# Attention of a two-layer kernel: heads placed in two halves of the rows, one DMA for the parts of a head, two groups projected at once, and all values at the beginning

## The reference

```
scores = q @ k.T * 16**-0.5          # (batch 2, head 16, 1024, 1024), causal
attn   = softmax(scores)
out    = (attn @ v) @ Wo (+ bo)
```

## Time and profile before

| | us |
|---|---|
| median of three runs | 2348.93 |
| profiled execution | 2359.97 |
| its span, first to last instruction | 2358.1 |
| granted TensorE clock, mean | 0.901 |

### The profile page before, as it was taken

One profiled execution on the slowest core, in us unless ns is written; L12 is line 12 of the kernel. 1 busy time (PEld: TensorE's weight loads), 2 busy tenths in 40 slices (PEclk: granted clock), 3 DMA queues, 4 the chain that ended last, 5 costly groups with the idle time before them and its releaser, 6 DMA issues. The chain is left out here.

```text
span 2358.1 us, 28715 instructions
## 1 busy us (share of the span) xinstructions
PE 1968.2 (83%) x9912; PEld 1308.5 (55%) x9912; DVE 1624.1 (69%) x3486; ACT 857.2 (36%) x1599; POOL 455.3 (19%) x324
## 2 busy tenths in 40 slices
PE   6899998699999988856867385646789999999998
PEld 4455554488888856433433242323345555469998
DVE  3788881444444354789999989996477888156775
ACT  2265563222222222430122111110325556336775
POOL 0011110623033030001101100110001111015775
PEclk9699998899999999978988697777869999989999
DMA  4122220311010010100000000000112222028885
GB/s 159 35 58 58 58 57 11 125 36 56 34 53 18 0 54 30 59 1 9 10 10 0 18 9 9 0 0 3 48 41 49 57 59 57 11 66 252 231 235 123
DMA packets 62849, 129.63 MB, mean 55 GB/s; under 512 B 22792, under 2 KB 33800, under 8 KB 59904
## 3 DMA queue, kind: packets, MB, share of 16 engines
q1 hardware_dynamic: 53120, 115.04, 16.3%
q0 software_dynamic: 8832, 12.16, 3.0%
q10 hardware_dynamic: 768, 0.79, 0.1%
HBM read 91.27 MB, written 10.98 MB: 43 GB/s over the span
## 5 line engine op out<-in xcount | busy, mean ns | idle before, releaser
L713 DVE CUSTOM_DVE_ANT_0 pair<-pair,a_mask 128x512 f32<-128x512 f32 (+3 forms) x768 | 409.6, 581 | 113.3 <-PE pair L561 110.1
L677 ACT ACTIVATE a_prob<-pair 128x512 f32<-128x512 f32 (+3 forms) x768 | 329.7, 496 | 248.6 <-PE pair L585 244.4
L561 PE MATMUL pair<-a_kx,a_qx 96*128 96x512 f32 (+3 forms) x768 | 255.2, 400 | 33.3 <-DMA a_qx<-a_comp 19.8
L585 PE MATMUL pair<-a_qx,a_kx 98*128 98x512 f32 (+3 forms) x768 | 267.3, 395 | 6.6 <-ACT a_prob L677 5.7
L956 DVE TENSOR_TENSOR m_h<-pair,m_g 128x512 f32<-128x512 f32 x96 | 66.4, 691 | 215.3 <-PE pair L779 214.6
L585 PEld LDWEIGHTS pair<-a_qx,a_kx 98*128 98x128 f32 x768 | 143.9, 194 | 118.6 <-ACT a_prob L677 81.2
L516 POOL TENSOR_SCALAR_AFFINE_SELECT a_prob<-a_prob 128x512 f32<-128x512 f32 x128 | 82.3, 643 | 644.8 <-ACT a_prob L677 644.8
L1338 PE MATMUL pair<-h_stream,r_w_kz 128*128 128x512 f32 x192 | 106.9, 712 | 116.6 <-DVE r_region L1744 113.3
L561 PEld LDWEIGHTS pair<-a_kx,a_qx 96*128 96x128 f32 x768 | 152.5, 205 | 91.6 <-DVE a_mx_raw L713 47.8
L777 PE MATMUL pair<-m_x_hi,m_w_lo 128*128 128x512 f32 x448 | 177.5, 396 | 26.4 <-POOL m_w_lo L841 24.2
L779 PE MATMUL pair<-m_x_lo,m_w_hi 128*128 128x512 f32 x448 | 176.3, 393 | 0.0
(11 more groups left out here) (307 smaller groups left out, 4126.9 us busy)
## 6 DMA issues: line engine op xcount, KB each, us to landing
mx_raw<-in_L_ffn_experts SPq DMA_DIRECT2D x69, 512.0 KB
m_raw<-in_L_cond_experts SPq DMA_DIRECT2D x18, 1024.0 KB, 4.8
a_kx<-a_comp SPq DMA_DIRECT2D x96, 128.0 KB, 2.4
a_qx<-a_comp SPq DMA_DIRECT2D x360, 32.0 KB, 2.0
a_factor<-a_inverses SPq DMA_DIRECT2D x56, 128.0 KB, 2.7
r_w_ring<-in_r_q_w SPq DMA_DIRECT2D x8, 512.0 KB, 4.0
m_raw<-in_L_cond_experts SPq DMA_DIRECT2D x6, 512.0 KB, 3.7
token_rows<-mx_h_rows SPq DMA_DIRECT2D x2, 1040.0 KB, 8.6
```

The source lines that it names most:

```text
L561: nc.tensor.matmul(first_bank[t % FR][:, 0:c1 - c0], qx[0:PRODUCT, m % 2, a, i * P:(i + 1) * P], kx[0:PRODUCT, m % 3, a // 2, c0:c1], star ...
L585: nc.tensor.matmul(score_bank[t % SR][:, q0:TT], kx[0:ROWS, n % 3, a // 2, j * P:(j + 1) * P], qx[0:ROWS, n % 2, a, h * TT + q0:(h + 1) * ...
L677: nc.scalar.activation(prob[:, i % RING, a, q0:TT], score_bank[t % SR][:, q0:TT], ACT.Exp, scale=SCALE).then_inc(s["b_exp"], 1)
L713: nc.vector.tensor_tensor_reduce(out=first_bank[t % FR][:, 0:cols], in0=first_bank[t % FR][:, 0:cols], in1=mask[:, m0:m0 + cols], scale=1. ...
```

## The change

Heads 0 and 2 of a group now lie in rows 0 to 63 of `qx` and `kx`, heads 1 and 3 in rows 64 to 127. Each has its three parts in 48 rows (50 with the maxima), with no zeros, and one DMA places the three parts of a head. For this `comp` holds four parts (upper, lower, upper, upper), of which ScalarE writes three, in two instructions. In the head, groups 0 and 1 are projected one after the other in banks of their own, the second through space of `prob`; group 0's keys are placed by half. All eight `v` blocks stand among group 0's 48 `first`, one behind every fifth, in four banks that are free there, and none is in a turn. ScalarE in place of VectorE copies values and maxima. The weight of the value matmul has 17 columns in place of 32. The ones of `kx` are set by GpSimd, before the keys come.

```diff
--- before.py
+++ after.py
-PRODUCT = 3 * 2 * HD
+VW = HD + 1
+PRODUCT = 3 * HD
 ROWS = PRODUCT + 2
...
-SMALL = (("max", 0, 1), None, None, ("qk", 2, 0), ("qk", 2, 1), ("max", 1, 0), ("v", 0, 0), None, None, None, None, None)
+SMALL = (("max", 0, 1), None, None, ("qk", 2, 0), ("qk", 2, 1), ("max", 1, 0), None, None, None, None, None, None)
...
 def before_turns():
 
     order = []
...
+        order += [("qk", 0, h), ("qk_use", 0, h), ("k_slots", 0, h), ("q_slots", 0, h)]
     for h in range(HALF):
-        order.append(("qk", 1, h))
-        firsts(MAX0 + 9 + 4 * h, MAX0 + 13 + 4 * h)
-        order.extend(finished("qk", 1, h))
-    firsts(MAX0 + 17, NF)
+        order += [("qk", 1, h), *finished("qk", 1, h)]
+    order.append(("q_slots", 1, 1))
+    values = [(pair, v) for pair in range(NG // 2) for v in range(2)]
+    for f in range(NF):
+        order.append(("first", 0, f))
...
+        if f % 5 == 2 and values:
+            order += [("v", *values[0]), ("v_use", *values[0])]
+            values = values[1:]
     order.append(("split", 0, 1))
     return order
...
+    early = {("qk", 0, 1): 0, ("qk", 1, 0): 1, ("qk", 1, 1): 2}
+    v_banks = [value_bank, *score_bank]
...
-        comp = c.sb(f"{tag}_comp", [P, 2, T], F32R, ctx=ctx)
+        comp = c.sb(f"{tag}_comp", [P, 4, T], F32R, ctx=ctx)
         kx = c.sb(f"{tag}_kx", [P, 3, PAIRS, T], F32R, ctx=ctx)
-        qx = c.sb(f"{tag}_qx", [P, 2, GH, T], F32R, ctx=ctx)
-        v_sb = c.sb(f"{tag}_v", [P, 4, QT, P], ctx=ctx)
+        qx = c.sb(f"{tag}_qx", [P, 2, PAIRS, T], F32R, ctx=ctx)
+        v_sb = c.sb(f"{tag}_v", [P, NG, QT, GH * VW], ctx=ctx)
...
+        second = prob[:, 0:2, :, :].rearrange("p x a t -> p (x a t)").rearrange("p (x t) -> p x t", x=4).bitcast(F32R)
+
+        def parts(m):
+            return second if m == 1 else comp[:, :, :]
+
+        def rows_of(a, n):
+            return slice(a % 2 * 64, a % 2 * 64 + n)
...
-                    for p in range(PAIRS):
-                        rows = slice(64 + p * 32, 96 + p * 32)
-                        for part, low in enumerate((0, 1, 0)):
-                            sp.dma_start(kx[part * 32:part * 32 + 32, m % 3, p, :].bitcast(F32), comp[rows, low, :].bitcast(F32))\
-                                .then_inc(s["k_in"], 16)
+                    t = slice(0, T) if h is None else half(h)
+                    for a in range(GH):
+                        rows = slice(64 + a * HD, 64 + a * HD + HD)
+                        sp.dma_start(kx[rows_of(a, PRODUCT), m % 3, a // 2, t].bitcast(F32), parts(m)[rows, 0:3, t].bitcast(F32))\
+                            .then_inc(s["k_in" if m else f"k_first{h}"], 16)
...
-                        for part, low in enumerate((0, 0, 1)):
-                            r0 = part * 32 + a % 2 * HD
-                            sp.dma_start(qx[r0:r0 + HD, m % 2, a, half(h)].bitcast(F32), comp[rows, low, half(h)].bitcast(F32))\
-                                .then_inc(s[f"q_in{h}"], 16)
+                        sp.dma_start(qx[rows_of(a, PRODUCT), m % 2, a // 2, half(h)].bitcast(F32),
+                                     parts(m)[rows, 1:4, half(h)].bitcast(F32))\
+                            .then_inc(s[f"q_in{h}" if m else f"q_first{h}"], 16)
...
-                    for a in range(GH):
-                        sp.dma_start(qx[PRODUCT:ROWS, m % 2, a, half(h)].bitcast(F32), stage[2 * a:2 * a + 2, :].bitcast(F32))\
+                    for x in range(2):
+                        sp.dma_start(qx[x * 64 + PRODUCT:x * 64 + ROWS, m % 2, :, half(h)].bitcast(F32),
+                                     stage[2 * PAIRS * x:2 * PAIRS * x + 2 * PAIRS, :].bitcast(F32))\
                             .then_inc(s[f"m_in{h}"], 16)
...
-                for a in range(GH):
-                    nc.gpsimd.memset(qx[:, 1, a, :].bitcast(F32), 0.0).then_inc(s["zero1"], 1)
...
+                for x in range(3):
+                    nc.gpsimd.memset(kx[:, x, :, :].bitcast(F32), 1.0).then_inc(s["ones"], 1)
...
-                    nc.tensor.matmul(first_bank[t % FR][:, 0:c1 - c0], qx[0:PRODUCT, m % 2, a, i * P:(i + 1) * P],
-                                     kx[0:PRODUCT, m % 3, a // 2, c0:c1], start=True, stop=True).then_inc(s["a_mm"], 1)
+                    r = rows_of(a, PRODUCT)
+                    nc.tensor.matmul(first_bank[t % FR][:, 0:c1 - c0], qx[r, m % 2, a // 2, i * P:(i + 1) * P],
+                                     kx[r, m % 3, a // 2, c0:c1], start=True, stop=True).then_inc(s["a_mm"], 1)
...
-                    nc.tensor.matmul(score_bank[t % SR][:, q0:TT], kx[0:ROWS, n % 3, a // 2, j * P:(j + 1) * P],
-                                     qx[0:ROWS, n % 2, a, h * TT + q0:(h + 1) * TT], start=True, stop=True)\
+                    r = rows_of(a, ROWS)
+                    nc.tensor.matmul(score_bank[t % SR][:, q0:TT], kx[r, n % 3, a // 2, j * P:(j + 1) * P],
+                                     qx[r, n % 2, a // 2, h * TT + q0:(h + 1) * TT], start=True, stop=True)\
                         .then_inc(s["b_mm"], 1)
...
-                        r = quadrant(a)
-                        last = nc.tensor.matmul(value_bank[r, q0:TT], v_sb[:, n % 4, j, r], prob[:, i % RING, a, q0:TT],
+                        r = slice(a * SLOT, a * SLOT + VW)
+                        last = nc.tensor.matmul(value_bank[r, q0:TT], v_sb[:, n, j, a * VW:(a + 1) * VW], prob[:, i % RING, a, q0:TT],
                                                 start=j == 0, stop=j == 4 * h + 3)
...
-                    nc.scalar.activation(comp[:, 0, half(h)], bank_of("qk", m, h), ACT.Copy).then_inc(s["hi"], 1)
...
+                    nc.scalar.activation(to[:, 2:4, :], bank_of("qk", m, h).unsqueeze(1).broadcast_to([P, 2, TT]), ACT.Copy)\
+                        .then_inc(s["hi"], 1)
+                    act.wait_ge(s["hi"], m * HALF + h + 1)
+                    nc.scalar.activation(to[:, 0, :], to[:, 2, :].bitcast(F32), ACT.Copy).then_inc(s["twin"], 1)
...
-                for a in range(GH):
-                    nc.vector.memset(qx[:, 0, a, :].bitcast(F32), 0.0).then_inc(s["zero0"], 1)
                 dve.wait_ge(s["mask"], 16)
```

More of the change, by code:

```diff
@@ L299, in turn @@
     closing = m == NG
-    order, found, uses = ([] if closing else [("q_slots", m, 1)]), 0, []
+    order, found, uses = ([("q_slots", m, 1)] if 1 < m < NG else []), 0, []
     for i in range(NS):
@@ L523, in take @@
                 def take(*entry):
-                    if used(*entry) > SB:
+                    if entry not in early and used(*entry) > SB:
                         pe.wait_ge(s["used"], used(*entry) - SB)
@@ L541, in v_projection @@
                     m = 2 * pair
-                    bank = take("v", pair, v)
+                    task = 2 * pair + v
+                    pe.wait_ge(s["used"], used("qk", 1, 1))
+                    if task >= len(v_banks):
+                        pe.wait_ge(s["v_used"], task - len(v_banks) + 1)
+                    bank = v_bank(pair, v)
                     for t in range(4):
@@ L648, in upper, with copy_values, copy_maxima @@
                     act.wait_ge(s["proj"], m * HALF + h + 1)
-                    if m and h == 0:
-                        act.wait_ge(s["k_in"], m * PAIRS * 3 * 16)
-                        act.wait_ge(s["q_in0"], m * GH * 3 * 16)
-                        act.wait_ge(s["q_in1"], m * GH * 3 * 16)
-                    nc.scalar.activation(comp[:, 0, half(h)], bank_of("qk", m, h), ACT.Copy).then_inc(s["hi"], 1)
+                    if m == 2 and h == 0:
+                        for x in range(HALF):
+                            act.wait_ge(s[f"k_first{x}"], GH * 16)
+                            act.wait_ge(s[f"q_first{x}"], GH * 16)
+                    if m > 2 and h == 0:
+                        for name in ("k_in", "q_in0", "q_in1"):
+                            act.wait_ge(s[name], (m - 1) * GH * 16)
+                    to = parts(m)[:, :, half(h)]
+                    nc.scalar.activation(to[:, 2:4, :], bank_of("qk", m, h).unsqueeze(1).broadcast_to([P, 2, TT]), ACT.Copy)\
+                        .then_inc(s["hi"], 1)
+                    act.wait_ge(s["hi"], m * HALF + h + 1)
+                    nc.scalar.activation(to[:, 0, :], to[:, 2, :].bitcast(F32), ACT.Copy).then_inc(s["twin"], 1)
+                def copy_values(pair, v):
+                    act.wait_ge(s["vp"], pair * 2 + v + 1)
+                    for x in range(2):
+                        last = nc.scalar.activation(
+                            v_sb[:, 2 * pair + x, 4 * v:4 * v + 4, :].rearrange("p t (a s) -> p t a s", s=VW)[:, :, :, 0:HD],
+                            v_bank(pair, v).rearrange("p (t x a s) -> p t x a s", t=4, x=2, s=HD)[:, :, x, :, :], ACT.Copy)
+                    last.then_inc(s["v_used"], 1)
+                def copy_maxima(m, h):
+                    act.wait_ge(s["t_mm"], m * HALF + h + 1)
+                    if h:
+                        act.wait_ge(s["m_in0"], (m + 1) * 2 * 16)
```

(11 more changed lines are left out.)

108 lines of the change are left out of this document (41 added, 67 removed).

## The result

The changed kernel takes 2405.51 us, the median of four runs, against 2352.66 before, the median of four. One of the four was disturbed (4644.01 us) and enters no ratio; the other three have 2390.92 to 2407.54, median 2403.47. The ratio is **1.022**, 95% interval 1.018 to 1.026: slower, where I had forecast 2258. The profiled execution took 2407.54, with a span of 2405.8 and a mean granted clock of 0.864, where it was 0.901.

A forecast was written before the change was run, and what follows sets the result against it. TensorE was taken to lead the turns, VectorE close behind at 31.3 of 37.2 us. Savings of 43.7 us in stage one and 47.7 in stage two, together 91.4, from the median 2348.93 gave 2258; range 2223 to 2300.

The forecast's parts named there:

- the likeness: Turns 1 to 5: would take 32.5 us, like the old turn 6 with TensorE 27.5 and VectorE 29.5 busy.
- TensorE then needs 32.9 - 1.8 - 4.6 = 26.5: Turns 1 to 5: TensorE's 32.9 us less 1.8 for the v projection and 4.6 for overlap, below VectorE's 29.2.
- First maximum: Head: VectorE's first maximum begins at 50.8 us, 6.1 us earlier.
- Rest of the head: Head after 50.8 us: 25.2 us of maxima, 0.9 of splits, 3.6 of waits; ends at 80.5 against 91.4.
- The rival with `v` blocks at half clock: Head: a v block takes 3.9 us, the sum loses 2 x 11 us, whole kernel 2280; chance 0.09.
- Turn 0: First turn of each stage: the 5.2 us wait for queries goes; about 33.5 us, 11 us less.
- VectorE's floor: Turns 1 to 5: VectorE busy 31.3 - 0.75 - 1.35 = 29.2 us a turn.
- Overlap of the halves: Turns: matmuls in opposite row halves run at once, 17.6 us become 13.0, 4.6 less, of which little is seen.
- The no-overlap rival: Turns: halves do not overlap, TensorE 31.1 us, turns 35.4, 54 us saved, whole kernel 2295; chance 0.17.
- Slower by bare weight loads: Turns: 44 same-half neighbours each pay a 0.19 us load, 8.4 a turn, turns about 43.8, whole kernel 2411; chance 0.05.
- Mode changes: Turns: TensorE switching between whole array and halves costs 0.085 us each, 0.34 a turn, within its slack.
- Closing turn: Last turn of each stage: no first there, each projection adds a change of tiling mode; +0.5 us.

The follow-up runs named there:

- e2: Kernel before the change, with first and scores stating 62 and 64 rows instead of 96 and 98, all in the lower half, no overlap; one execution, 2421.94 us.
- e5: Changed kernel, halves kept, with 62 and 64 rows stated instead of 48 and 50; 2330.23 us in one execution, 2333.43 as median of five, ratio 0.991.
- e12: e1 with first stated over 126 rows instead of 96 and scores over 128 instead of 98, zeros or ones between; 2307.8 us, ratio 0.981.
- e1: Changed kernel without halves: 96 and 98 rows over the whole array as before, with the earlier part layouts, zeros and DMAs; 2314.79 us, ratio 0.983.
- e9: e5 with each q/k projection moved one place on, away from right behind a value block, and the maxima one step later; 2333.78 us, ratio 0.990.
- e10: e5 with six of the eight v blocks back in the turns; 2330.78 us, ratio 0.990.
- e4: Changed kernel with 32 weight columns for the values instead of 17 in the first attention stage alone; one execution, 2399.5 us.
- e8: e1 with six of the eight v blocks back in the turns; 2323.04 us, ratio 0.987.

## Why the prediction was wrong

**The failed step** is the sentence under turns 1 to 6 that takes 32.5 us from turn 6 of the old kernel as the likeness: that turn ran at 1.00, and I held the clock for a property of how full TensorE is. The sum has no term for a clock lost inside the turns. I wrote of whole-clock V blocks "TensorE is nearly filled between blocks", and named a half clock inside the turns only as what would make me wrong, with no chance of its own. The rows stated fell by half, and the clock with them. What shows it: e2 (fewer rows, no halves, turn 4 at 0.92), e5 (the change with more rows, 1.00), e12 (e1 with more rows, turn 6 from 0.86 to 1.00), three pairs in which nearly all of the work and its order stay. The cost of the term, by e5 against the change, is 36.0 us in the first stage and 39.0 in the second.

**The second step that failed** is the price of a turn at the whole clock. For the first stage my sum gives 338.5 us (382.2 - 43.7); the change takes 411.0 and e5 375.0, so stating more rows gives back only half of the 72.5. Of e5's 36.5 us above the sum, turn 0, still at 0.78, is 8.1; turns 1 to 5, of which three have the whole clock, are 19.3, the rest of the head 8.2, closing 1.5, and the first maximum and turn 6 -0.7. The turns rest on "TensorE then needs 32.9 - 1.8 - 4.6 = 26.5". It is busy for 33.2 to 33.5 in e5's turns at 1.00, and for 34.2 in e1's, without overlap: the overlap took about 1 us off its busy time and not 4.6, and the 32.9 was low before that, since the earlier trace rows has TensorE busy for 36.3 us of each of turns 2 to 5. So TensorE never fell below VectorE, and the likeness with turn 6, which has no projection, did not hold.

**Point by point.**
- First maximum: +11.7 us forecast, +11.4 measured. Right.
- Rest of the head: 29.7 us forecast to the end of group 0's splits (50.8 to 80.5), 42.7 measured (48.5 to 91.2). The sum took less, a saving of 2.4 from the first maximum on; measured are 8.1 lost. The rival with `v` blocks at half clock (0.09) had the price right, 3.9 for the 3.79 us of the first block, and a loss near its 11 us came, 10.5 against the sum, but not by its path: three blocks of eight ran so, which is 5 us. In e12, with its first block alone at 3.78 and the clock at 0.93, the same stretch takes 36.7, still 7.0 above my figure: up to the last maximum (35.2 us) VectorE, busy 25.3 of it, stands idle for 9.9, where I had reckoned 3.6 behind the eight blocks.
- Turn 0: the queries' wait is gone, as said. 33.5 forecast, 42.9 at 0.75, and 34.6 in e12 at 1.00. The step was right but for the clock and 1 us.
- VectorE's floor: 29.2 forecast, 28.6 to 29.7 busy in e5's turns 1 to 5. Right.
- Overlap of the halves: right as a mechanism, worth nothing in turns 1 to 5. The no-overlap rival gave 35.4 a turn (its stage two should read 3.9 us more and not 2.2, with turn 1 at 39.4, so 2294); e5, with overlap and whole clock, has 35.5, and e1, without, 34.4 to 35.6. In turn 6 it is worth what I said: 30.5 forecast, 30.1 in e5. The difference is the projections. VectorE idles 2.05 us in e5's turn 6 (30.1 - 28.05) and 5.95 in its turn 3 (35.6 - 29.65): 3.9 more, of which 1.29 and 2.18 stand right behind the two projections of 1.98. Three banks do not carry VectorE over them. Had the clock held, the change would thus still have missed 2258: e5's turns are 3 us above my 32.5. e9 moved them and gained 0.6 (34.9), with VectorE's waits behind them as long as before. What would take away the rest, 2.4 us a turn, is not tested.
- Slower by bare weight loads: it gave 2411, close to the 2405.5, by coincidence. e5 has the same loads and halves at 35.5 a turn, so the mechanism did not act. The Trainium skill (TensorE: Matmul & The Clock Gate, The mechanism) has loads overlap a running matmul only where the row group differs; e5's 35.5 us a turn, where the rival has 43.8, speaks against paying for it here.
- Mode changes: e5 contains them, and turn 6 with its maxima blocks takes 30.1 there, 0.4 less than forecast; no run shows a price for them. Closing turn: +0.5 forecast, +3.8 measured at 0.84, and -3.2 in e12 at 0.95.

**The sum in hindsight.** In stage one of e12 against before: until the first maximum -4.1, rest of the head +1.9, turn 0 -9.8, turn 1 -2.0, turns 2 to 5 -7.5, turn 6 +0.7, closing -3.2: -24.0. These are the moves of work that the change also holds, but for the placement in halves, at the clock that it lost.

**Left open.** Why turns of one form differ (0.79 to 0.95) in one execution; why turn 0 stays near 0.8 at 62 and 64 rows in halves, whether `v` blocks are in the turns or not (e10); how far the 17 columns add to it at 48 rows (e4 was one execution); and whether halves in turn 6 alone, where they give 1.4 to 3.1 us (30.1 against e8's 31.5 and e12's 33.2), could be had on top of e12. That was not tried.

## What to carry to other kernels

Read the granted clock by stretch before a matmul is made to touch fewer rows, and forecast with a term for it: here it was at least half of the miss. Much of the rest is that a busy engine's need was added up from single prices, 32.9 us, and not checked against its busy row, 36.3. A contraction that leaves rows unused can be stated over all of them with zeros on one side, at no time of its own. And an overlap on one engine is worth only what its partners, a few banks behind, can take.
